# First attention of a two-layer kernel: the causal mask of the score tiles moves from TensorE matmuls into VectorE's row maximum of the diagonal tiles

## Chip, cores and metric

The kernel runs on one core of one Trainium2 chip, as one program. The metric is the device time of one execution in microseconds; the figure is the median of several runs. TensorE (PE in the profile) multiplies, VectorE (DVE) and ScalarE (ACT) work element by element, GpSimd (POOL) does element-wise work, masks and some transfers, SyncE (SP) issues most transfers.

## The reference, cut to what matters

Two layers stand in a row. Each computes `x + s * silu(g)`, with s an attention of the normalised x and g a feed-forward part. In the first layer s is a linear attention, and g holds a whole transformer block with a causal softmax attention of 16 heads of 16 dimensions, followed by a mixture of 8 experts. B is 2, T is 2048 and D is 256 there. That softmax attention is the "first attention" of the title:

```python
q, k = (rope(q), rope(k))
scores = jnp.einsum('bqhd,bkhd->bhqk', q, k) / math.sqrt(hd)
causal = jnp.tril(jnp.ones((Tt, Tt), dtype=bool))
scores = jnp.where(causal, scores, jnp.asarray(-1000000000.0, scores.dtype))
probs = jax.nn.softmax(scores, axis=-1)
attn = jnp.einsum('bhqk,bkhd->bqhd', probs, v).reshape(Bb, Tt, d) @ Wproj
```

The second layer has a causal attention too, of 16 heads of 32 dimensions.

## The kernel before, in words

The program's stages follow one another: projections for both attentions of layer one (`project_first`), the first attention (`narrow_attention`, L233), the expert layer, the projections of layer two, and the second attention (`wide_attention`, L763), which runs into the output.

**The work of the first attention.** The 2 x 16 heads are cut into 8 groups of 4 heads (HG). The 2048 queries are cut into 4 blocks of 512 (QB). A unit (g, u) is one group and one query block; its keys are blocks 0 to u. There are 32 units. For each unit two passes over the scores are made:

- *Score tiles* ("S", `score_tile`, L423): 128 queries on the partitions against up to 512 keys, written to one of three buffers `s_ps` (one bank each). VectorE takes the maximum over the keys (L393), which frees the buffer (`item_free`). Of a unit there are 4 x 4 x (u + 1) such tiles, 1280 in all. A tile with j == u is diagonal: it has only (qt + 1) x 128 columns, and its last 128 columns are cut by the causal mask. 512 tiles are diagonal, 128 of each width. The planner orders them by query tile, pair of heads, key block j and then head, so that the two diagonal tiles of a pair of heads follow one another. After a unit's tiles, "M" (L400 to L408) makes from the partial maxima a shift in two halves, and "T" transposes it into a strip which SyncE writes under the queries as two more rows.
- *Key tiles* ("ST", `key_tile`, L442): 128 keys on the partitions against the 512 queries, two heads per item, with the shift included. ScalarE takes the exponentials (L368), and "PV" (L510) multiplies them with the values: eight matmuls in single precision for four heads.

Two heads lie on partitions 0 to 49 and 64 to 113 (`heads_down` = 2), so matmuls of two heads use different rows of the array.

**The masks.** TensorE adds the causal mask itself. After the scores of a diagonal tile it multiplies an identity with a mask of -1e30 and adds into the last 128 columns, in two halves of 64 rows within the head's own half of the array:

```python
for half in range(2):
    wide = slice(64 * (1 - half), 64 * (1 - half) + P)
    mm = pe.matmul(place[:, width - P:width], ident_wide[rows, wide],
                   mask_wide[rows, wide], start=False, stop=half == 1)
```

Key tiles get theirs in the same way (L458) from `back_wide`. The wide masks are made by GpSimd in `NarrowMasks.make` (L218), long before the stage, and the constants in `make_constants` (L1138) at the start of the program.

The second attention treats its score tiles otherwise: there VectorE adds the mask `later` and takes the maximum in one instruction, `tensor_tensor_reduce` (L966), which appears in the trace as two records, an operation on the tile and a read of the accumulator.

**The order.** `narrow_schedule` (L62) writes out the order of all items ahead of time, and every engine follows it: TensorE issues S, ST and PV in the order of `body`, VectorE takes S, M and T in their order, and so on. It is made by a small model with costs per item: the start of each possible next item is computed, and the earliest goes next, an S item with a bonus of 100 ns. In this model a matmul costs 0.417 ns a column, a mask 110 ns, and a row maximum takes 1.04 ns a column plus 25 when VectorE is behind, or plus 125 after the tile's end plus 220 when it is idle (L160).

## Time and profile before

| | us |
|---|---|
| median of 3 runs (lowest, highest) | 3019.21 (3013.8, 3020.83) |
| span of the profiled execution, first to last instruction | 3006.4 |
| median of the runs above that span | 12.8 |
| the first attention, from its first row maximum to its last | 260 to 1041 |

The profiled execution has no time of its own beside its span; the 12.8 us lie before the first and after the last instruction of the program, or are the difference between executions. The profile lists busy time of each engine as the union of its records. A record runs from the start of an instruction to its modelled end, and records of successive instructions on one engine can overlap: the next may start before the record of the one before has ended. PEld are the weight loads of TensorE. PEclk is the share of TensorE's full clock that was granted.

### The profile page before, as it was taken

How to read it: one execution, taken by the hardware profiler on the slowest of the kernel's cores; microseconds unless marked ns; L12 is line 12 of the kernel's file. 1: busy time of each engine (PE TensorE's matmuls, PEld its weight loads, DVE VectorE, ACT ScalarE, POOL GpSimd, SP SyncE). 2: the span in 40 equal slices, each digit the busy share in tenths (PEclk: the TensorE clock that was granted, in tenths of full speed). 3: DMA queues.
4: the chain of work that ended last, by engine and by line, in shares of the span. 5: the costliest groups of instructions: out<-in, count | busy, mean ns of one | idle time of the engine just before them, and what ended most of it. 6: DMA issues, size and time to landing. Idle time of an engine off the chain costs nothing. (4 is left out here: it accounts for less than half of the span.)

```text
span 3006.4 us, 46248 instructions
## 1 busy us (share of the span) xinstructions
PE 2831.9 (94%) x18017; PEld 1317.3 (44%) x18017; DVE 2010.2 (67%) x4329; ACT 1545.3 (51%) x2581; POOL 990.0 (33%) x533
## 2 busy tenths in 40 slices
PE   7998999999999976999999899899999999999999
PEld 4664233333333344666676545323333333333327
DVE  7887899999999845000000565688787877878823
ACT  3452477676777755222222444345565665565571
POOL 1000000110101103111101330157777777777791
PEclk9997899999999987999999999889999999999999
DMA  4322122133202124232111466312020220202103
GB/s 130 97 77 76 37 51 39 43 62 66 50 24 62 24 68 130 63 86 75 63 48 34 148 193 185 79 32 61 8 64 12 68 64 8 64 12 68 67 12 119
DMA packets 141306, 200.77 MB, mean 67 GB/s; under 512 B 14320, under 2 KB 107904, under 8 KB 138000
## 3 DMA queue, kind: packets, MB, share of 16 engines
q1 hardware_dynamic: 130672, 173.21, 20.9%
q0 software_dynamic: 9056, 24.59, 3.9%
q8 instruction: 143, 2.34, 0.3%
q14 instruction: 75, 0.61, 0.1%
q10 hardware_dynamic: 1360, 0.01, 0.0%
HBM read 121.21 MB, written 76.02 MB: 66 GB/s over the span
## 5 line engine op out<-in xcount | busy, mean ns | idle before, releaser
L946 ACT ACTIVATE at_probs<-at_st 128x512 f32<-128x512 f32 (+3 forms) x1280 | 588.5, 542 | 442.1 <-PE at_st L1040 282.4
L909 POOL TENSOR_TENSOR at_probs<-at_probs 128x2048 f32<-128x2048 f32 (+3 forms) x205 | 725.9, 3546 | 214.7 <-ACT at_probs L946 135.4
L393 DVE TENSOR_REDUCE at_part<-at_s 128x1 f32<-128x512 f32 (+3 forms) x1280 | 690.0, 603 | 63.0 <-PE at_s L431 28.6
L368 ACT ACTIVATE at_probs<-at_st 128x1024 f32<-128x1024 f32 (+3 forms) x640 | 541.6, 895 | 275.4 <-PE at_st L450 141.0
L972 DVE TENSOR_REDUCE at_part<-at_s 128x1 f32<-128x512 f32 x768 | 498.5, 683 | 67.8 <-PE at_s L1032 63.9
L966 DVE CUSTOM_DVE_ANT_0 at_s<-at_s,at_later 128x384 f32<-128x384 f32 (+3 forms) x512 | 246.9, 498 | 103.8 <-PE at_s L1032 102.4
L510 PE MATMUL at_acc<-at_probs,at_v 128*32 128x512 f32 (+3 forms) x2560 | 305.5, 551 | 8.2 <-ACT at_otile L355 7.8
L2358 DVE TENSOR_TENSOR ex_ot<-ex_bank,lin_b 128x512 f32<-128x512 f32 x32 | 22.2, 692 | 426.3 <-PE ex_bank L2388 352.2
L2321 ACT ACTIVATE ex_hT<-ex_bank,ex_b 128x512 f32<-128x512 f32 x128 | 87.9, 687 | 334.7 <-PE ex_bank L2378 332.7
L2378 PE MATMUL ex_bank<-ex_xT,lin_w 128*128 128x512 f32 x512 | 225.5, 598 | 1.0 <-ACT ex_xT L2314 1.0
L2388 PE MATMUL ex_bank<-lin_w,ex_hT 128*128 128x256 f32 x1024 | 223.7, 379 | 0.8 <-ACT ex_hT L2321 0.8
L1032 PE MATMUL at_s<-all_k,all_q 96*128 96x512 f16 (+3 forms) x640 | 199.4, 366 | 15.1 <-DVE at_part L972 6.1
L2388 PEld LDWEIGHTS ex_bank<-lin_w,ex_hT 128*128 128x128 f32 x1024 | 193.9, 190 | 31.1 <-issue 3.8
L1040 PE MATMUL at_st<-all_q,all_k 98*128 98x512 f16 (+3 forms) x640 | 194.9, 362 | 6.6 <-ACT at_probs L946 3.8
L1032 PE MATMUL at_s<-at_kT,at_qT 96*128 96x512 f16 (+3 forms) x640 | 192.3, 356 | 8.3 <-DVE at_part L966 3.8
L431 PE MATMUL at_s<-lin_k_first,lin_q_first 48*128 48x512 f16 (+3 forms) x640 | 184.6, 374 | 14.9 <-DVE at_part L393 5.8
L1040 PE MATMUL at_st<-at_qT,at_kT 98*128 98x512 f16 (+3 forms) x640 | 185.1, 350 | 8.3 <-ACT at_probs L946 6.8
L431 PE MATMUL at_s<-at_kT,at_qT 48*128 48x512 f16 (+3 forms) x640 | 176.4, 361 | 6.9 <-DVE at_part L393 4.2
L1864 POOL DMA_DIRECT2D att_sums<-att x28 | 14.5, 523 | 487.7 <-DMA att<-at_otile 487.7
L2549 POOL DMA_INDIRECT p_rows<-exp_out,all_gather_at x64 | 62.1, 970 | 270.3 <-PE p_rot L2731 182.3
L2378 PEld LDWEIGHTS ex_bank<-ex_xT,lin_w 128*128 128x128 f32 x512 | 98.2, 192 | 118.2 <-issue 117.5
L1094 PE MATMUL at_acc<-at_probs,at_v 128*32 128x512 f32 (+3 forms) x1280 | 144.4, 536 | 4.0 <-ACT at_otile L928 3.8
(342 smaller groups left out, 3950.0 us busy)
## 6 DMA issues: line engine op xcount, KB each, us to landing
att<-at_otile SPq DMA_DIRECT2D x64, 256.0 KB, 2.1
lin_w<-in_W SPq DMA_DIRECT2D x16, 1024.0 KB, 7.5
at_v<-v SPq DMA_DIRECT2D x11, 1024.0 KB, 11.1
v<-pr_vt SPq DMA_DIRECT2D x32, 256.0 KB
exp_out<-ex_ot SPq DMA_DIRECT2D x32, 256.0 KB, 2.1
v<-p_vt SPq DMA_DIRECT2D x32, 256.0 KB, 3.7
p_xs<-in_x SPq DMA_DIRECT2D x8, 512.0 KB, 5.2
qhi<-p_parts SPq DMA_DIRECT2D x8, 512.0 KB
```

What stands on the lines that cost most here:

```text
L368: act.activation(probs[:, quad % RING, heads_down * p:heads_down * (p + 1), off:QB], st_ps[n % st_slots][:, :, off:QB], ACT.Exp, scale=EXP ...
L393: dve.tensor_reduce(part[:, w % 2, qt * HG + h, j:j + 1], s_ps[n % S_SLOTS][:, 0:width], AX.X, ALU.max).then_inc(item_free, 1)
L431: mm = pe.matmul(place[:, 0:width], QT[g % 2][rows, h // heads_down, q0:q0 + P], KT[g % 2][rows, h // heads_down, j * QB:j * QB + width], ...
L510: mm = pe.matmul(acc_ps[32 * h:32 * h + 32, off:QB], V[g % 2][:, kc, 32 * h:32 * h + 32], probs[:, quads % RING, h, off:QB], start=kc == 0 ...
L909: pool.tensor_tensor(total, total, probs[:, slots.slot[quad], :, off:QB], ALU.add).then_inc(add_done, 1)
L946: act.activation(probs[:, slots.slot[quad], h, off:QB], st_ps[n % ST_SLOTS][:, off:QB], ACT.Exp, scale=EXP_SCALE).then_inc(exp_done, 1)
L966: dve.tensor_tensor_reduce(out=s_ps[n % S_SLOTS][:, 0:width], in0=s_ps[n % S_SLOTS][:, 0:width], in1=later[:, QB - width:QB], scale=1.0, s ...
L972: dve.tensor_reduce(part[:, w % 2, qt * HG + h, j:j + 1], s_ps[n % S_SLOTS][:, 0:width], AX.X, ALU.max).then_inc(item_free, 1)
L1032: pe.matmul(place[:, 0:width], QT[g % 2][0:K, h, q0:q0 + P], KT[g % 2][0:K, h, j * QB:j * QB + width], start=True, stop=True).then_inc(ite ...
L1040: mm = pe.matmul(place[:, off:QB], KT[g % 2][0:K + 2, h, kc * P:(kc + 1) * P], QT[g % 2][0:K + 2, h, u * QB + off:(u + 1) * QB], start=Tru ...
L2378: mm = pe.matmul(d[:, :], w1[e % 2][:, n, f * P:(f + 1) * P], xT[:, n, cb * QB:(cb + 1) * QB], start=n == 0, stop=n == NF - 1)
L2388: mm = pe.matmul(d[:, t * D:(t + 1) * D], hT[cb][:, n, (2 * m + t) * P:(2 * m + t + 1) * P], w2[e % 2][:, n, :], start=n == 0, stop=n == N ...
```

## The change

The two mask matmuls of every diagonal score tile are left out. VectorE's row maximum of a diagonal tile becomes one `tensor_tensor_reduce`, which adds `later` (zeros, with -1e30 above the diagonal in its last 128 columns) to the tile in place and takes the maximum. Other tiles keep `tensor_reduce`. VectorE waits once, at the start of the stage, until the masks are made. The tile `mask_wide` and the constant `mask_qk` are not made any more (`mask_qk` was read by nothing), `later` is made in their place, and the counts of the semaphores follow. The key tiles' masks stay. In the planner, the 110 ns of a diagonal tile's mask go, and VectorE's cost, for plain and diagonal tiles alike, becomes 1.04 ns a column plus 125 after the later of the tile's end plus 220 and the end of VectorE's last item less 60: 1.04 ns a column plus 65 where VectorE is behind.

```diff
@@ -154,10 +154,10 @@
                 row_at[ev[1]] = dve + 2500
             else:
                 of_unit = of_unit + 1 if of_unit < count[ev[1]] else 1
-                end = start + ev[5] * COLUMN + (110 if ev[4] == ev[1][1] else 0)
+                end = start + ev[5] * COLUMN
                 issue, rows[ev[3] % heads_down] = start + 30, end
                 pe = max(pe, end)
-                dve = max(dve + ev[5] * 1.04 + 25, end + 220 + ev[5] * 1.04 + 125)
+                dve = max(dve - 60, end + 220) + ev[5] * 1.04 + 125
             slot_free[n_item % s_slots] = dve
             n_item += 1
             if at < len(ahead) and ahead[at][0] == "M":
@@ -212,16 +212,21 @@
 
 class NarrowMasks:
     def __init__(self, c):
-        self.tiles = [c.sb(n, [P, 3 * P // 2], BF16) for n in ("ident_wide", "mask_wide", "back_wide")]
+        self.tiles = [c.sb(n, [P, 3 * P // 2], BF16) for n in ("ident_wide", "back_wide")]
+        self.later = c.sb("later", [P, QB], BF16)
         self.cleared, self.ready = c.sem("masks_cleared"), c.sem("masks_ready")
 
     def make(self, pool):
-        for wide in self.tiles:
-            pool.memset(wide[:, :], 0.0).then_inc(self.cleared, 1)
+        for tile in (*self.tiles, self.later):
+            pool.memset(tile[:, :], 0.0).then_inc(self.cleared, 1)
         pool.wait_ge(self.cleared, 3)
+        last = self.later[:, QB - P:QB]
+        pool.affine_select(out=last, in_=last, compare_op=ALU.is_ge, fill=MASK, base=0, pattern=[[-1, P]],
+                           channel_multiplier=1).then_inc(self.ready, 1)
+        pool.wait_ge(self.ready, 1)
         for y in range(2):
-            for wide, compare, fill, base, step in zip(self.tiles, (ALU.not_equal, ALU.is_ge, ALU.is_ge),
-                                                       (1.0, MASK, MASK), (64, 64, -64), (-1, -1, 1)):
+            for wide, compare, fill, base, step in zip(self.tiles, (ALU.not_equal, ALU.is_ge),
+                                                       (1.0, MASK), (64, -64), (-1, 1)):
                 part = wide[64 * y:64 * y + 64, :]
                 pool.affine_select(out=part, in_=part, compare_op=compare, fill=fill, base=base,
                                    pattern=[[step, 3 * P // 2]], channel_multiplier=-step).then_inc(self.ready, 1)
@@ -380,6 +385,7 @@
         def _(dve):
             n, w = 0, 0
             due = []
+            dve.wait_ge(masks.ready, 5)
             for ev in body:
                 if ev[0] == "EV" and ev[1] == last_unit[ev[1][0]] and ev[1][0] + 1 < GROUPS:
                     due.append([ev[1][0], LATER])
@@ -389,9 +395,13 @@
                         A.invert(dve, due.pop(0)[0])
                 if ev[0] == "S":
                     _, (g, u), qt, h, j, width = ev
+                    place, to = s_ps[n % S_SLOTS][:, 0:width], part[:, w % 2, qt * HG + h, j:j + 1]
                     dve.wait_ge(item_ready, n + 1)
-                    dve.tensor_reduce(part[:, w % 2, qt * HG + h, j:j + 1],
-                                      s_ps[n % S_SLOTS][:, 0:width], AX.X, ALU.max).then_inc(item_free, 1)
+                    if j == u:
+                        dve.tensor_tensor_reduce(out=place, in0=place, in1=masks.later[:, QB - width:QB], scale=1.0,
+                                                 scalar=MASK, op0=ALU.add, op1=ALU.max, accum_out=to).then_inc(item_free, 1)
+                    else:
+                        dve.tensor_reduce(to, place, AX.X, ALU.max).then_inc(item_free, 1)
                     n += 1
                 elif ev[0] == "M":
                     g, u = ev[1]
@@ -423,20 +433,12 @@
             def score_tile(ev, n):
                 _, (g, u), qt, h, j, width = ev
                 q0 = u * QB + qt * P
-                diagonal = j == u
                 place = s_ps[n % S_SLOTS]
                 if n >= S_SLOTS:
                     pe.wait_ge(item_free, n - S_SLOTS + 1)
                 rows = slice(base(h), base(h) + K)
                 mm = pe.matmul(place[:, 0:width], QT[g % 2][rows, h // heads_down, q0:q0 + P],
-                               KT[g % 2][rows, h // heads_down, j * QB:j * QB + width],
-                               start=True, stop=not diagonal)
-                if diagonal:
-                    rows = slice(base(h), base(h) + 64)
-                    for half in range(2):
-                        wide = slice(64 * (1 - half), 64 * (1 - half) + P)
-                        mm = pe.matmul(place[:, width - P:width], ident_wide[rows, wide],
-                                       mask_wide[rows, wide], start=False, stop=half == 1)
+                               KT[g % 2][rows, h // heads_down, j * QB:j * QB + width], start=True, stop=True)
                 mm.then_inc(item_ready, 1)
 
             def key_tile(ev, n):
@@ -1127,20 +1129,20 @@
 def constants(nc, c, shift_rows):
 
     C = {"ident16": c.sb("ident16", [P, P], BF16), "ident_f16": c.sb("ident_f16", [P, P], F16),
-         "identf": c.sb("identf", [P, P], F32), "mask_qk": c.sb("mask_qk", [P, P], BF16),
+         "identf": c.sb("identf", [P, P], F32),
          "mask_kq": c.sb("mask_kq", [P, P], BF16), "ones32": c.sb("ones32", [P, 32], F32), "onesf": c.sb("onesf", [P, P], F32),
          "ones16": c.sb("ones16", [P, P], BF16), "tri16": c.sb("tri16", [P, P], BF16),
          "shift_rows": shift_rows, "const_ready": c.sem("const_ready")}
-    C["const_count"] = 15
+    C["const_count"] = 13
     return C
 
 
 def make_constants(pool, C):
-    for k in ("ident16", "ident_f16", "identf", "mask_qk", "mask_kq"):
+    for k in ("ident16", "ident_f16", "identf", "mask_kq"):
         pool.memset(C[k][:, :], 0.0).then_inc(C["const_ready"], 1)
     for k in ("ones32", "onesf", "ones16", "tri16"):
         pool.memset(C[k][:, :], 1.0).then_inc(C["const_ready"], 1)
-    pool.wait_ge(C["const_ready"], 9)
+    pool.wait_ge(C["const_ready"], 8)
 
     pool.affine_select(out=C["tri16"][:, :], in_=C["tri16"][:, :], compare_op=ALU.is_ge,
                        fill=0.0, base=0, pattern=[[1, P]],
...
@@ -1150,14 +1152,10 @@
                            fill=1.0, base=0, pattern=[[-1, P]],
                            channel_multiplier=1).then_inc(C["const_ready"], 1)
 
-    pool.affine_select(out=C["mask_qk"][:, :], in_=C["mask_qk"][:, :], compare_op=ALU.is_ge,
-                       fill=MASK, base=0, pattern=[[-1, P]],
-                       channel_multiplier=1).then_inc(C["const_ready"], 1)
-
     pool.affine_select(out=C["mask_kq"][:, :], in_=C["mask_kq"][:, :], compare_op=ALU.is_ge,
                        fill=MASK, base=0, pattern=[[1, P]],
                        channel_multiplier=-1).then_inc(C["const_ready"], 1)
-    pool.wait_ge(C["const_ready"], 15)
+    pool.wait_ge(C["const_ready"], 13)
 
 
 NT = B * T // P
```

The two hunks that are not shown drop `mask_wide` where `masks.tiles` is unpacked, and change the count that TensorE waits for from 6 to 5.

## Rows read from the trace of the kernel before

**Rows 1.** The page: busy time by engine, granted clock in 40 slices.

```profile
PE 2831.9 (94%) x18017; PEld 1317.3 (44%) x18017; DVE 2010.2 (67%) x4329; ACT 1545.3 (51%) x2581; POOL 990.0 (33%) x533
...
PEclk9997899999999987999999999889999999999999
```

**Rows 2.** Stretches: us, PE, PEld, DVE, ACT, POOL, PEclk, DMA share, GB/s.

```profile
400.00:500.00 100.00, 97.22 (x925) 35.74 (x924) 92.87 (x186) 69.50 (x85) 11.70 (x17) 1.00 0.25 50
500.00:600.00 100.00, 98.23 (x958) 37.50 (x960) 93.64 (x185) 71.17 (x87) 11.40 (x17) 1.00 0.25 50
...
700.00:800.00 100.00, 98.27 (x936) 36.83 (x936) 92.61 (x184) 70.88 (x86) 11.40 (x17) 0.98 0.25 50
...
260.00:1045.00 785.00, 758.55 (x6959) 281.53 (x6958) 721.44 (x1415) 522.34 (x630) 80.56 (x122) 0.96 0.23 46
```

**Rows 3.** Timeline of TensorE around 610 us: start, us, engine, line, what.

```profile
610.23 0.28 PE L431 MATMUL at_s<-at_kT,at_qT 48*128 48x256 f16 x1
610.35 0.27 PE L438 MATMUL at_s<-lin_mask_wide,lin_ident_wide 64*128 64x128 bf16 x2
```

**Rows 4.** Waits in 260 to 1045 us: who waited for whom, total, times, longest.

```profile
PEld at_s L431 <- DVE at_part L393: 328.2, 650, 1.7
...
DVE at_part L393 <- PE at_s L431: 28.6, 48, 2.0
DVE at_part L393 <- PE at_s L438: 23.2, 55, 4.9
```

**Rows 5.** By form, 255 to 1050 us: count, busy, mean ns, idle before.

```profile
L393 DVE TENSOR_REDUCE at_part<-at_s 128x1 f32<-128x512 f32 x896 | 562.7, 683 | 38.3 <-PE at_s L431 24.3 <-PE at_s L438 7.2
...
L438 PE MATMUL at_s<-lin_mask_wide,lin_ident_wide 64*128 64x128 bf16 x1024 | 133.2, 224 | 0.0
...
L438 PEld LDWEIGHTS at_s<-lin_mask_wide,lin_ident_wide 64*128 64x128 bf16 x1024 | 88.3, 99 | 25.3 <-issue 2.6
L393 DVE TENSOR_REDUCE at_part<-at_s 128x1 f32<-128x384 f32 x128 | 64.8, 548 | 4.3 <-PE at_s L438 4.1
...
L393 DVE TENSOR_REDUCE at_part<-at_s 128x1 f32<-128x256 f32 x128 | 48.6, 417 | 7.5 <-PE at_s L431 4.3 <-PE at_s L438 1.3
...
L393 DVE TENSOR_REDUCE at_part<-at_s 128x1 f32<-128x128 f32 x128 | 32.8, 284 | 13.0 <-PE at_s L438 10.6
```

**Rows 6.** Busy time by stretch, early in the stage, columns as in rows 2.

```profile
260.00:380.00 120.00, 109.21 (x781) 39.47 (x776) 104.24 (x204) 48.39 (x59) 1.77 (x4) 0.75 0.19 41
320.00:330.00 10.00, 8.34 (x35) 2.91 (x36) 8.89 (x19) 2.70 (x4) 0.00 (x0) 0.50 0.04 16
```

**Rows 7.** Timeline of VectorE, plain row maxima of the first attention.

```profile
312.42 7.27 DVE L393 TENSOR_REDUCE at_part<-at_s 128x1 f32<-128x512 f32 x12 [0.33 <-PE at_s L431]
...
876.93 0.68 DVE L393 TENSOR_REDUCE at_part<-at_s 128x1 f32<-128x128 f32 x3
```

**Rows 8.** Timeline of VectorE, masked row maxima of the second attention.

```profile
2234.08 0.69 DVE L966 CUSTOM_DVE_ANT_0 at_s<-at_s,at_later 128x512 f32<-128x512 f32 x1
2234.68 0.14 DVE L966 DVE_READ_ACCUMULATOR2_ANT at_part<- 128x1 f32 x1
2234.68 1.88 DVE L972 TENSOR_REDUCE at_part<-at_s 128x1 f32<-128x512 f32 x3
...
1908.67 0.73 DVE L966 CUSTOM_DVE_ANT_0 at_s<-at_s,at_later 128x512 f32<-128x512 f32 x1
1909.32 0.14 DVE L966 DVE_READ_ACCUMULATOR2_ANT at_part<- 128x1 f32 x1
1909.32 0.73 DVE L966 CUSTOM_DVE_ANT_0 at_s<-at_s,at_later 128x512 f32<-128x512 f32 x1
```

**Rows 9.** Timeline of GpSimd: a select of the constants, the last of the masks.

```profile
3.35 0.28 POOL L1153 TENSOR_SCALAR_AFFINE_SELECT all_mask_qk<-all_mask_qk 128x128 bf16<-128x128 bf16 x1
...
38.33 0.39 POOL L226 TENSOR_SCALAR_AFFINE_SELECT lin_back_wide<-lin_back_wide 64x192 bf16<-64x192 bf16 x1
```

**Rows 10.** One line's instructions: ns min/median/max, first and last start in us.

```profile
L393 DVE TENSOR_REDUCE at_part<-at_s x1280: 279/681/693, 260.2 to 1040.6; 128x1 f32<-128x512 f32 x127, 128x1 f32<-128x256 f32 x21, 128x1 f32<-128x128 f32 x19, 128x1 f32<-128x384 f32 x16
```

More of the change, by code:

```diff
@@ L260, in narrow_attention @@
         otile = c.sb("otile", [P, 2, QB], F32)
-        ident_wide, mask_wide, back_wide = masks.tiles
+        ident_wide, back_wide = masks.tiles
         st_ps = [c.ps(f"st{k}", [P, heads_down, QB]) for k in range(st_slots)]
@@ L462, in _ @@
             pe.wait_ge(C["const_ready"], C["const_count"])
-            pe.wait_ge(masks.ready, 6)
+            pe.wait_ge(masks.ready, 5)
             n = pairs = quads = 0
```

## Prediction, made before the changed kernel was run

> **What bounds the kernel now.** I read the page first: its slices and its busy shares say that TensorE is the fullest engine of the whole [rows 1]. Its chain of waits is of no use here: its lines are those of the second attention and of the end. So the first attention was cut out with the stretches. In 260 to 1045 us TensorE is busy 758.55 of 785 us and VectorE 721.44; ScalarE has 522.34 and GpSimd 80.56 [rows 2]. Two engines are nearly full, and the question is which one leads. TensorE's busy time overstates it, because a matmul's record outlasts its share of the array: in the example at 610 us the mask's record starts 0.12 us after a matmul whose own record is 0.28 us long [rows 3]. The waits settle it. The weight load of a score tile waits 650 times, 328.2 us together, for VectorE's row maximum to free one of the three score buffers, while VectorE waits for a score tile 48 + 55 times, 51.8 us in all [rows 4]. So VectorE leads: TensorE stands at the head of its queue until a buffer comes free, and VectorE stops only now and then, when the score tile was late. The planner's body alternates about four score tiles with two key tiles and one product with V, and eight matmuls of such a product cannot be interrupted. From the shapes, the stage gives VectorE 896 reductions of 512 columns and 128 of each narrower width [rows 5].
>
> **The change, part by part.**
>
> *TensorE's masks.* 1024 matmuls and 1024 weight loads leave, two for each of the 512 diagonal tiles [rows 5]. What counts is by how much a tile is ready earlier. In the example the tile's own matmul ends at 610.23 + 0.28 = 610.51 and its masks at 610.35 + 0.27 = 610.62 [rows 3]: 0.11 us. Since VectorE leads, this is worth something only where VectorE was waiting. Lower bound: the 55 waits that ended on a mask [rows 4], 55 x 0.11 = 6.1 us. Upper bound: diagonal tiles come in pairs (two heads), so in front of each of the 103 waits two of them may have pushed back what TensorE issued later: 103 x 2 x 0.11 = 22.7 us. I take the upper one, for two reasons. Where VectorE's records overlap by 0.085 us (below), waits shorter than that are not counted among the 103, and they shrink too. And at half clock (260 to 380 us has a granted clock of 0.75 on average [rows 6]) each mask costs double.
>
> *VectorE's plain reductions.* 12 of 512 columns in a row last 7.27 us, one 0.683: (7.27 - 0.68) / 11 = 0.60 us from start to start; three of 128 columns give (0.68 - 0.28) / 2 = 0.20 [rows 5, 7]. The next one starts 0.085 us before the end of the one before.
>
> *VectorE's diagonal tiles.* The new instruction is the one that the second attention already uses, on the same shapes, so its rows stand for it. It is two records, the operation and a read of the accumulator (0.14 us). Alone between reductions: started 2234.08, next reduction started 2234.68, 0.60, and the three reductions from there last 1.88 = 2 x 0.60 + 0.68: about 0.01 us more before and after at most [rows 8]. Behind another of its kind: 1908.67 to 1909.32, 0.65, so 0.05 more than 0.60 [rows 8]. For the 24 units with u > 0 that is 8 pairs each: 192 x (0.01 + 0.05 + 0.01) = 13.4 us. In the 8 units with u = 0 all 16 tiles are diagonal and follow one another: 8 x (0.01 + 15 x 0.05 + 0.01) = 6.2 us. The 32 row maxima (L400) also wait for the last accumulator read: between 0 and 32 x 0.14 = 4.5 us, taken at the middle, 2. Together **21.6 us** more work on the leading engine. From both sides: 13 (all singles and pairs at 0.04) to 24.
>
> What does a rule make of this? The row shows the accumulator read and the next operation starting at the same time, 1909.32 and 1909.32 [rows 8]. The Trainium skill (VectorE: DVE Perf Modes, "The DRAIN you can't avoid") says that the next operation does not start until the pipe of the one before is empty, and counsels few operations rather than fused ones. Read strictly it would make each diagonal tile cost the full 0.73 + 0.14 us instead of 0.65; the rows do not agree. The sum does not use it; it returns as a rival.
>
> *The buffer comes free later.* A reduction frees it after 0.68 us, the new pair of records after 0.60 + 0.14 = 0.74 (0.65 + 0.14 = 0.79 behind its like) [rows 8]. Waiting for that is TensorE's next score matmul but two, and behind it in the same queue the key tiles (so ScalarE's exponentials) and the products. As three buffers are in use, 0.06 to 0.11 us matter only where VectorE runs dry: at most 103 x 0.07 = 7.2 us. Against it, at the same waits, the tiles queued in front last 0.07 us longer on VectorE if a pair is among them, which hides as much: 103 x 0.07 = 7.2. I set the two off.
>
> *The order.* The planner's VectorE was 1.04 ns a column plus 25 when full, 0.557 us for 512 columns; the trace has 0.60. The changed formula gives 1.04 ns plus 65, 0.597. So the whole body is laid out anew with a truer VectorE for plain tiles (and 0.05 too fast for paired diagonal ones, and without their later release). No row shows what an order is worth. The nearest are the hundreds of the present one, each with other pieces of the pattern: VectorE is busy between 92.61 and 93.64 of 100 us [rows 2], 1.03 a hundred, or 8 us over 785. I take 0, from -8 to +8.
>
> *Preparation.* GpSimd loses one fill and one select of the constants (the select 0.28 us) and, in the masks, two selects for one (one of that kind takes 0.39), with a wider fill and one more wait; the last of them ends at 38.7 us [rows 9], and VectorE's new wait for `masks.ready` stands at 260 us. No DMA is added or moved, so no queue of SP or GpSimd is passed. Cost 0; were the cover gone, under 1 us.
>
> **Sum.** 21.6 - 22.7 = -1.1 us against the span of 3006.4 us. The median of the three runs is 3019.2, 12.8 more than the profiled span; that difference stays. So 3018 us. What a measurement of this kernel can tell from no change is about 0.2%, 6 us.
>
> **The rivals.**
>
> *Faster: the waits shrink more than that.* If the new cover hides (7.2) without the later release biting, and the truer order brings its 8: -1.1 - 7.2 - 8 = -16.3, **3003 us**. For it: VectorE's visible idle time is 785 - 721.44 = 63.6 us, and TensorE becomes looser by a good part of the masks' busy 133 us. Against: VectorE's own work is a floor that rises by 21.6.
>
> *Slower: VectorE leads and TensorE's relief is worth little.* Place: the row of diagonal tiles in each unit. If only the 55 mask-ended waits shrink, 21.6 - 6.1 = +15.5, **3035 us**. It decides from the point where less than 21.6 - 6 = 15.6 us of waiting disappears. For it: 650 waits of TensorE for VectorE against 103 the other way. Against: most waits of VectorE stand behind a product with V, with diagonal tiles just before, and these now take less of TensorE.
>
> *Slower: the clock.* In 320 to 330 us the granted clock is 0.50, the lower of the two levels (1.2 GHz), with TensorE busy 8.34 of 10; the hundreds with 97 to 98 have 0.98 to 1.00 [rows 2, 6]. With less to do TensorE could stay at the lower level longer. Price from either level: 204 VectorE operations in 120 us is 0.588 us each, and 186 in 100 us is 0.538, so 9%: one more such stretch of 120 us is worth 10 us, 3028. The Trainium skill (TensorE: Matmul & The Clock Gate, "What's actually happening") has activity release the throttle; the trace agrees that the fuller stretches have the full clock.
>
> *The strict rule on emptying.* Each diagonal tile would take its whole record and the read after it: at 512 columns 0.69 to 0.73, say 0.70, and 0.14 [rows 8], so 0.24 us over a reduction's 0.60, and as much at the other widths, x 512 = 123 us, 3141. The rows speak against it.
>
> *The change does not do what it says:* masks that ran wholly beside other matmuls free nothing. That is the slower rival with 21.6 instead of 15.5, 3041, and is counted there.
>
> **How the numbers follow.** Cancelling, as forecast: 0.42 (of it 0.02 beyond the bound on either side). Faster: 0.36. VectorE's bound: 0.17. Clock: 0.04. Strict rule: 0.01. So faster by over 0.2%: 0.36 + 0.02 = 0.38; within: 0.38; slower: 0.17 + 0.04 + 0.01 + 0.02 = 0.24. Both signs hold much, so the forecast's own range is given too: 3018 - 8 to 3018 + 8 for the order, 3010 to 3026. The range for 8 in 10 reaches to the faster rival, 3003, and most of the way to the slower one, 3033.
>
> **What would show each step.** Gone: all 1024 mask matmuls. VectorE: 512 pairs of records in place of as many reductions, 0.60 us apart at 512 columns alone and 0.65 behind one another; if the second is 0.60, 10 us of the cost were not real. Waits of VectorE for a score tile in the stage: from 51.8 us to about 30 as forecast; below 20 the faster rival, above 40 the slower one. Waits of TensorE's weight load for VectorE should grow from 328 us, since TensorE gets looser. The stage's start, 260 us, stays; its last row maximum over a score tile, now at 1040.6 [rows 10], tells the change by itself. The rest of the kernel should move as a block: any difference there is not of this change. The forecast is wrong if the stage moves by more than 8 us either way.

## The result, and the profile after

The changed kernel takes 3035.4 us (median of four runs, 3035.3 to 3041.1), the one before 3017.0 us in its four: the ratio is 1.0071, 95% interval 1.0056 to 1.0086. It is 18 us slower, 2 us above the range that was given. It fell where the slower rival had been put (3035). That the number agrees is luck: VectorE got less added work than that rival has (16.9 us and not 21.6), its waits grew where the rival lets them shrink, and some 8 us came back at the stage's end. Two executions in the batch of a5 and a6, one of a5 at 5298.8 us and one of the kernel before at 10281.7 us, lie far outside the others and are in no ratio below.

One correction to the frame comes first. The profiled execution of the changed kernel took 3035.48 us for a span of 3033.7, so only 1.8 us lie around a span; in the kernel before it is 2.1 (one of its executions has 3008.55 us for a span of 3006.4). By that, the execution of the kernel before that was profiled (span 3006.4) took some 3008.5 us, and was one of its fastest: its runs beside the later experiments lie between 3008.6 and 3022.7. The 12.8 us that the prediction took to be around the span were mostly difference between executions. So the traces, 27.3 us apart, show 9 us more than the medians do.

The page of the changed kernel, busy shares and granted clock in 40 slices:

```profile
PE 2830.3 (93%) x16993; PEld 1268.7 (42%) x16993; DVE 2032.9 (67%) x4841; ACT 1544.8 (51%) x2581; POOL 989.7 (33%) x530
...
PEclk9997799999999897999999899899999999999999
```

The 1024 matmuls are gone, and VectorE has 512 records more (the accumulator reads). The span grew in the first attention: its last row maximum ends at 1073.7 us instead of 1041.3, its last eviction at 1107.5 instead of 1083.5, and the second attention starts 27.0 us later and takes 1102.7 instead of 1102.4 us. The 8 us between the first two differences come back at the stage's end: from the last row maximum to the last eviction it takes 33.9 us instead of 42.2. That belongs to the order: the kernels below in the changed order have 33 to 35 us there, those in the former order 41 to 43, as the changed order leaves less key work behind the last score tile.

Stretches of the changed kernel (us, PE, PEld, DVE, ACT, POOL, PEclk, DMA share, GB/s), to be laid beside [rows 2]:

```profile
260.00:1078.00 818.00, 762.84 (x5998) 233.55 (x5997) 743.84 (x1927) 530.62 (x639) 81.86 (x123) 0.90 0.22 44
400.00:500.00 100.00, 92.89 (x750) 28.80 (x748) 89.15 (x222) 67.47 (x82) 11.68 (x17) 0.90 0.25 48
500.00:600.00 100.00, 94.36 (x795) 29.94 (x792) 93.33 (x244) 69.45 (x85) 11.42 (x17) 0.95 0.25 51
700.00:800.00 100.00, 94.40 (x788) 29.86 (x788) 92.97 (x243) 69.32 (x84) 11.40 (x17) 0.93 0.26 50
```

The granted clock in the stage is 0.90 where it was 0.96, and it is 0.90 to 0.95 in hundreds that had 0.98 to 1.00 [rows 2]. Summed over the trace's records of the clock, the stage has 169 us at the lower level instead of 74.

The waits of the changed kernel in 260 to 1078 us:

```profile
PEld at_s L440 <- DVE at_part L404: 248.8, 435, 1.7
PEld at_s L440 <- DVE at_part L401: 141.8, 306, 1.7
DVE at_part L404 <- PE at_s L440: 36.9, 61, 2.2
...
DVE at_s L401 <- PE at_s L440: 25.3, 48, 4.8
```

VectorE's visible waits are 62.2 us in 109 times, against 51.8 in 103 [rows 4]. They were to fall to 30. TensorE's weight load waits 390.6 us for VectorE instead of 328.2, as expected from a looser TensorE.

VectorE's records at the end of the stage, start and duration in us:

```profile
1058.21 0.69 DVE L401 CUSTOM_DVE_ANT_0 at_s<-at_s,lin_later 128x512 f32<-128x512 f32 x1
1058.81 0.14 DVE L401 DVE_READ_ACCUMULATOR2_ANT at_part<- 128x1 f32 x1
1058.81 0.73 DVE L401 CUSTOM_DVE_ANT_0 at_s<-at_s,lin_later 128x512 f32<-128x512 f32 x1
1059.46 0.14 DVE L401 DVE_READ_ACCUMULATOR2_ANT at_part<- 128x1 f32 x1
1059.46 1.28 DVE L404 TENSOR_REDUCE at_part<-at_s 128x1 f32<-128x512 f32 x2
```

From one start to the next it is 0.60 for the first of a pair, 0.65 for the second, and 0.60 for the plain ones after it (1.28 less 0.68): the distances of [rows 8], to the hundredth.

**Work and waits of VectorE.** For all that follows the stage was split by VectorE's records. The least distance from one start to the next is 598, 465, 332 and 198 ns for plain tiles of the four widths, 8 more for a masked one, 51 more for a masked one behind another, 7 more for a plain one behind it, and fixed values for the small operations. What a start comes later than that is a wait; the rest is work. The order of VectorE's own items is the same in every kernel here (but for the seven divisions by the sums), so any two can be compared item by item. What the two "orders" differ in is where TensorE puts the score tiles between its key tiles and products.

| kernel | masks on TensorE | row maximum | order | median us | ratio to before, 95% | work | waits | low clock |
|---|---|---|---|---|---|---|---|---|
| before | yes | plain | former | 3017.0 | 1 | 705.2 | 79.5 | 74 |
| changed | no | masked | changed | 3035.4 | 1.0071 (1.0056 to 1.0086) | 722.1 | 93.0 | 169 |
| a4_fill_old | load only | masked | former | 3036.1 | 1.0063 (1.0039 to 1.0088) | 723.1 | 84.2 | 99 |
| a1_ttr_old | no | masked | former | 3041.8 | 1.0099 (1.0081 to 1.0118) | 724.7 | 87.1 | 150 |
| a5_none_old | no | plain | former | 3013.2 | 0.9993 (0.9982 to 1.0004) | 706.6 | 77.0 | 116 |
| a6_none_new | no | plain | changed | 3030.5 | 1.0046 (1.0030 to 1.0062) | 707.0 | 99.8 | 173 |
| a2_red_new | yes | plain | changed | 3054.1 | 1.0140 (1.0122 to 1.0158) | 705.2 | 126.0 | 154 |
| a3_fill_new | load only | masked | changed | 3059.2 | 1.0156 (1.0139 to 1.0173) | 722.1 | 116.2 | 150 |

Work and waits in us from the first row maximum over a score tile to the end of VectorE's last copy of the stage (1.6 to 4.6 us after the last such maximum); low clock in us at 1.2 GHz up to the last eviction. "Load only" means that TensorE does the mask matmuls but the scores overwrite them. The ratios are each to the kernel before in the same batch. Every kernel has one profile here, and a profile differs from the next by up to 10 us, as the repeats below show.

### The profile page after: what moved, and what is told of

It is laid out like the page before. It is cut to its first block and busy times, and to the rows that moved or that the text cites. A ratio compares the mean times of both kernels' runs of the same rounds, so it can differ in the third digit from the quotient of the medians.

```text
span 3033.7 us, 44708 instructions
## 1 busy us (share of the span) xinstructions
PE 2830.3 (93%) x16993; PEld 1268.7 (42%) x16993; DVE 2032.9 (67%) x4841; ACT 1544.8 (51%) x2581; POOL 989.7 (33%) x530
## 5 line engine op out<-in xcount | busy, mean ns | idle before, releaser
L974 DVE TENSOR_REDUCE at_part<-at_s 128x1 f32<-128x512 f32 x768 | 498.4, 683 | 68.2 <-PE at_s L1034 64.3
L404 DVE TENSOR_REDUCE at_part<-at_s 128x1 f32<-128x512 f32 x768 | 484.4, 684 | 42.1 <-PE at_s L440 36.9
L512 PE MATMUL at_acc<-at_probs,at_v 128*32 128x512 f32 (+3 forms) x2560 | 315.6, 565 | 7.4 <-ACT at_otile L360 7.4
L401 DVE CUSTOM_DVE_ANT_0 at_s<-at_s,lin_later 128x384 f32<-128x384 f32 (+3 forms) x512 | 242.5, 510 | 29.6 <-PE at_s L440 25.3
L440 PE MATMUL at_s<-lin_k_first,lin_q_first 48*128 48x512 f16 (+3 forms) x640 | 192.5, 389 | 27.6 <-DVE at_part L404 16.9
L440 PE MATMUL at_s<-at_kT,at_qT 48*128 48x512 f16 (+3 forms) x640 | 186.0, 381 | 16.6 <-DVE at_part L404 12.1
L1096 PE MATMUL at_acc<-at_probs,at_v 128*32 128x512 f32 (+3 forms) x1280 | 144.4, 536 | 4.0 <-ACT at_otile L930 3.8
```

The lines of the kernel that those rows point to most:

```text
L404: dve.tensor_reduce(to, place, AX.X, ALU.max).then_inc(item_free, 1)
L440: mm = pe.matmul(place[:, 0:width], QT[g % 2][rows, h // heads_down, q0:q0 + P], KT[g % 2][rows, h // heads_down, j * QB:j * QB + width], ...
L512: mm = pe.matmul(acc_ps[32 * h:32 * h + 32, off:QB], V[g % 2][:, kc, 32 * h:32 * h + 32], probs[:, quads % RING, h, off:QB], start=kc == 0 ...
L974: dve.tensor_reduce(part[:, w % 2, qt * HG + h, j:j + 1], s_ps[n % S_SLOTS][:, 0:width], AX.X, ALU.max).then_inc(item_free, 1)
L1096: mm = pe.matmul(acc_ps[32 * h:32 * h + 32, off:QB], V[g % 2][:, kc, 32 * h:32 * h + 32], probs[:, slots.slot[quads], h, off:QB], start=kc ...
```

## The experiments

Three theories were set against one another. W: VectorE's added work sets the time. O: the order that the changed planner writes costs it. C: TensorE, relieved of the masks, gets the lower clock for longer. The change has three parts (masks off TensorE, masked row maximum, order), and the first six experiments make the other six combinations of them.

**a1_ttr_old**: the changed kernel with the former planner.

```diff
-                dve = max(dve - 60, end + 220) + ev[5] * 1.04 + 125
+                dve = max(dve + ev[5] * 1.04 + 25, end + 220 + ev[5] * 1.04 + 125)
```

(and the 110 ns of a mask back in `end`.)

> The changed kernel, but with the order of the kernel before (its planner put back). Theory W (VectorE's 20 us of added work set the time): 3035, as the changed kernel. Theory O (the new order costs it): back to 3017, within 5. Theory C (without the masks TensorE's granted clock falls in a stretch of every group): it depends on whether this order also leaves TensorE a thin stretch; if it does, some stretches of 10 us at 0.5 and about 3030; if not, the clock is 0.99 to 1.00 in 400 to 1000 us and the time is 3017 to 3022.

3041.8 us. O falls as it stood: giving the changed kernel its former order back does not return its loss. By the medians that order is even 6 us worse for it (ratios 1.0099 and 1.0071, whose intervals just overlap).

**a2_red_new**: the kernel before with the changed planner; the diff above the other way round.

> The kernel before (masks on TensorE, plain row maxima), but in the order of the changed planner. Theory W: 3017, since VectorE's work is the old one. Theory O: 3030 or more, most of the loss is there. Theory C: the masks keep TensorE occupied, so the clock stays near 1.00 in 400 to 1000 us and the time is within 5 of 3017.

3054.1 us, 42 above its batch's kernel before. W and C, which gave 3017 within 5, fall here. So for the kernel before, the changed order is far worse: 46.5 us more waits for the same work. Its waits of VectorE for score tiles:

```profile
DVE at_part L393 <- PE at_s L438: 50.9, 77, 4.9
DVE at_part L393 <- PE at_s L431: 47.0, 77, 2.2
```

97.9 us against 51.8 [rows 4]. What an order is worth is not a matter of 8 us. The lower clock comes with the order too: 154 us instead of 74, although TensorE has all its masks.

**a3_fill_new** and **a4_fill_old**: the changed kernel and a1, in which TensorE does the two mask matmuls of each diagonal tile ahead of the scores, which overwrite them.

```diff
+                if j == u:
+                    rows = slice(base(h), base(h) + 64)
+                    for half in range(2):
+                        wide = slice(64 * (1 - half), 64 * (1 - half) + P)
+                        pe.matmul(place[:, width - P:width], ident_wide[rows, wide],
+                                  back_wide[rows, wide], start=half == 0, stop=half == 1)
```

> The changed kernel with two mask matmuls ahead of each diagonal score tile, whose result the scores overwrite: TensorE has its old load again, VectorE keeps the new one. Theory C: the clock returns to 0.98 to 1.00 in 400 to 1000 us and the time falls below the changed kernel's 3035, to about 3022. Theory W: 3035 plus up to 22 for the later tiles, 3035 to 3057. Theory O: 3035 or more.

> The same two overwritten mask matmuls, changed VectorE work, and the order of the kernel before: only VectorE's instruction on diagonal tiles differs from the kernel before. Theory W: 3017 + 20 = 3037. Theory O: 3017. Theory C: clock near 1.00, 3017 plus what VectorE's added work costs by itself, between 5 and 20.

a3 takes 3059.2 us, 24 more than the changed kernel, and its low stretches stay (150 us): in the changed order they do not come from the missing masks. a4 differs from the kernel before in VectorE's instruction and in that the mask matmuls stand ahead of the scores instead of behind them: 17.9 us more work, 4.7 more waits, and 3036.1 us against 3012.2 in its batch. That is W's term in the former order, and it is as large as the loss of the whole change (1.0039 to 1.0088 against 1.0056 to 1.0086). In the changed order the same term is much smaller, as a6 shows.

**a5_none_old** and **a6_none_new**: neither mask (plain row maxima over unmasked diagonal tiles, with sums floored so that the output stays finite), in both orders.

```diff
+        dve.tensor_scalar(self.sums[:, :], self.sums[:, :], 1.0e-30, None, ALU.max).then_inc(self.floored, 1)
+        dve.wait_ge(self.floored, g + 1)
         dve.reciprocal(self.sums[:, :], self.sums[:, :]).then_inc(self.inverted, 1)
```

> Neither the two mask matmuls nor the masked row maximum: plain row maxima over unmasked diagonal tiles (so the shift may come from a later key, and the sums are floored at 1e-30), order of the kernel before. It shows what taking the masks off TensorE does alone. Theory C (less load on TensorE brings the lower clock): low stretches spread over the stage as in the run with the old order and the masked maximum, no gain, 3012 to 3022. Theory G (the relief is worth its 22 us and VectorE's work ate it): 2990 to 2998.

> The same without both masks, in the changed planner's order, which has in each group one run of 11 score tiles with no key tile and no product between. Against the changed kernel it leaves out VectorE's added work alone. Theory W: 20 us below the changed kernel, 3015. Theory C: also about 3015, but with one low stretch of 10 to 14 us in each group at the same places.

a5: 3013.2 us, ratio 0.9993 with an interval that holds 1 (0.9982 to 1.0004, so at most 5 us gained). In the former order, taking all masks off TensorE's score tiles gains nothing that can be told; VectorE pays only 1.4 us for it, the seven floors of the sums. The 22 us that its expectation calls theory G are not there. VectorE's one kind of wait there:

```profile
DVE at_part L393 <- PE at_s L431: 51.5, 78, 4.7
```

51.5 us against 51.8 before [rows 4]: fewer, and longer. Item by item against the kernel before, 104 of the items at full clock in both wait 17.5 us less (the relief is real), 50 wait 13.8 us more, and the items that fell into a low stretch wait 8.2 instead of 2.1, while those that came out of one wait 4.0 less. It is more than chance: between the first profile of the kernel before and its repeats, 4 or 5 items at full clock wait 1 to 2 us less and 8 to 10 wait 3 to 5 more.

a6 takes 3030.5 us with 173 us at low clock, where both W and C had 3015. In it VectorE waits 72.9 us:

```profile
DVE at_part L393 <- PE at_s L431: 72.9, 125, 4.7
```

So the changed order costs 17 us over a5 (ratios 0.9993 and 1.0046) with no mask anywhere, and the masked row maxima, 15.1 us more work on top of it, only 5 us more by the medians and 8 by the ratios (1.0046 and 1.0071), as waits fall from 99.8 to 93.0.

The eight kernels together say that the three parts do not add. What each part adds to the time, in per cent, from the ratios (each has an interval of 0.1 to 0.25 to either side):

| part | in which kernels | former order | changed order |
|---|---|---|---|
| masked row maximum | masks still on TensorE | +0.63 | +0.16 |
| masked row maximum | masks off TensorE | +1.06 | +0.25 |
| masks off TensorE | plain row maximum | -0.07 | -0.94 |
| masks off TensorE | masked row maximum | +0.36 | -0.85 |

The changed order adds 1.40 (masks on, plain), 0.93 (load only, masked) and 0.53 (no mask), and takes 0.28 off in the whole change. So the loss of 0.71% has no single owner: which part seems to bring it depends on the part that one starts with.

**b1_runfill_after**, **b2_runfill_red_new**, **b3_prefill_after** try to hold the clock by filling TensorE. Reading the two orders as written showed what stands where the changed one has a low stretch in each group: it has, in groups 1 to 7, a run of 9 to 11 score tiles with no key tile and no product with V between, while the former order has none past group 0 or 1. Key tiles of a unit need its row maxima turned and stored; in the changed order the key tiles have caught up (lead 1.67 units on average against 1.88), and nothing else is left to do. In the changed kernel's timeline the run looks so (chosen records):

```profile
648.57 0.23 PE L440 MATMUL at_s<-at_kT,at_qT 48*128 48x128 f16 x1 [0.25 <-DVE at_part L401]
...
649.84 0.23 PE L440 MATMUL at_s<-at_kT,at_qT 48*128 48x128 f16 x1 [1.05 <-DVE at_part L404]
...
652.17 0.28 PE L440 MATMUL at_s<-at_kT,at_qT 48*128 48x128 f16 x1 [0.49 <-DVE at_part L404]
...
654.80 1.03 PE L452 MATMUL at_st<-at_qT,at_kT 50*128 50x512 f16 x4 [0.24 <-DMA at_qT<-at_strip]
...
655.51 1.02 ACT L373 ACTIVATE at_probs<-at_st 128x1024 f32<-128x1024 f32 x1 [10.24 <-PE at_st L452]
```

ScalarE had nothing for 10.24 us. The stretches around it:

```profile
640.00:650.00 10.00, 8.38 (x86) 3.26 (x86) 9.60 (x23) 3.29 (x7) 0.00 (x0) 1.00 0.01 2
650.00:660.00 10.00, 7.77 (x36) 2.19 (x35) 9.17 (x28) 4.26 (x5) 2.36 (x5) 0.53 0.23 76
660.00:670.00 10.00, 9.88 (x62) 2.15 (x54) 7.69 (x21) 5.88 (x7) 5.08 (x5) 0.78 0.25 33
```

By the trace's records of the clock it falls to 1.2 GHz at 650.7 us, within the run, and is back at 664.4. In the run itself VectorE is busy 9.17 to 9.60 of 10: it loses little there. The key tiles come at 654.8, still at the lower clock. In 660 to 670 us, of which 4.4 are at the lower clock (0.78 on average), TensorE is busy 9.88 and VectorE only 7.69.

```diff
+                if n in filled:
+                    for x in range(4):
+                        pe.matmul(place[:, x * P:(x + 1) * P], C["ident16"][:, :], C["mask_kq"][:, :],
+                                  start=True, stop=True)
```

`filled` holds the tiles of the runs in b1 and b2, and in b3 the 512-column plain ones among the 12 items before a run.

> The changed kernel with four idle matmuls of 128 columns, overwritten by the scores, ahead of each score tile of the runs of 11 in groups 1 to 7, where TensorE only waits for VectorE. Theory C: the low stretch of each group after that run (7 of 10 to 14 us) goes, the clock in 400 to 1000 us is 0.98 or more, and the time falls by 8 to 20 us, to 3015 to 3027. If the clock is not what costs, the time stays at 3035 or rises by up to 5 while the clock recovers.

> The same filling in the kernel before with the changed order (3054 without it). Theory C: clock 0.98 or more in 400 to 1000 us and 3025 to 3040. If the order costs by its interleaving and not by the clock, it stays at 3050 or more.

> The changed kernel with four idle matmuls of 128 columns, overwritten by the scores, ahead of the plain 512-column score tiles among the 12 items before each run of score tiles without key tiles. There VectorE has two wide tiles queued, so the 0.21 us each should hide, unlike in the run itself, where it showed in full. Theory C: the low stretches near 450, 550, 650 us and so on (10 to 14 us each, 7 of them) vanish or shorten, VectorE's waits at low clock fall from 38 us by 10 to 17, and the time from 3035 to 3018 to 3026. Theory O alone: the clock recovers and the time stays at 3033 to 3038.

3051.7, 3059.4 and 3062.7 us: all worse, and none does what it was for. In b1 the low stretches stay (169 us), and the filling runs at the lower level:

```profile
658.39 0.61 PE L452 MATMUL at_s<-all_mask_kq,all_ident 128*128 128x128 bf16 x4
658.93 0.10 PEld L455 LDWEIGHTS at_s<-at_kT,at_qT 48*128 48x128 f16 x1 [0.20 <-issue]
658.93 0.28 PE L455 MATMUL at_s<-at_kT,at_qT 48*128 48x128 f16 x1
659.14 0.35 PEld L452 LDWEIGHTS at_s<-all_mask_kq,all_ident 128*128 128x128 bf16 x4
...
660.01 0.30 DVE L401 CUSTOM_DVE_ANT_0 at_s<-at_s,lin_later 128x128 f32<-128x128 f32 x1 [0.40 <-PE at_s L455]
```

Four idle matmuls take 0.54 us before each score matmul (658.39 to 658.93), more than VectorE spends on a narrow tile, so it waits. b3 adds 26 us of waits at full clock. b2 does lift the clock (101 us low instead of 154) but pays for it with the filling. By b2's expectation a time over 3050 would speak for the interleaving and against the clock. But as tests of the clock all three failed: filling a tile's own path is not free, and what it costs cannot be told from what the clock gives back. So no experiment here separates the price of the long runs from that of the lower clock behind them.

**c1_ttr_own40**, **c2_red_dve60**, **c3_ttr_no110** are other orders: c1 and c3 for the changed work, c2 for the kernel before. c1 adds 40 ns for a diagonal tile to the former formula, c3 only drops the 110 ns of the masks, c2 takes the changed VectorE formula and keeps them.

> The changed kernel's work in an order from the former planner with 40 ns added for each diagonal tile and the 110 ns of the mask kept, as if TensorE still had it. This order keeps the lead of the score tiles at 1.87 units (former order 1.88, changed one 1.67) and has no run of over 5 score tiles. Theory C: as the changed work in the former order, thin load spread over the stage, 120 to 150 us at low clock, 3035 to 3042. If the order's fit to VectorE's added work matters more than the clock: 3025 to 3032.

> The kernel before, whose planner gets the changed formula for VectorE but keeps the 110 ns of the masks. With both changed it took 3054. If the loss there came from planning without masks that TensorE still had to do, 3015 to 3025 here; if it came from the VectorE formula (lead 1.72, runs of 9 score tiles), 3040 to 3055.

> The changed kernel's work in an order from the former VectorE formula without the 110 ns of the masks: the planner knows TensorE's lighter load and believes VectorE 7% faster than it is. Lead 1.77, one run of 9 at the end. Theory C: fewer and shorter low stretches than the changed kernel's 169 us, 100 to 140, and 3022 to 3032. Theory W alone: 3035.

3049.5, 3046.1 and 3038.4 us. c2 says that most of a2's loss (waits 116.2 us where a2 has 126.0 and the kernel before 79.5) comes with the VectorE formula, though this formula is the truer one by [rows 7]. c1 kept the lead at 1.87 and had no long run, and still had 186 us at low clock, spread in 3 to 17 us pieces: the run is one way to the lower clock, not the only one. c1 came out 7 us above what its expectation allowed, and c3 (159 us at low clock) missed the 3022 to 3032 of C. Four orders were tried on the masked row maximum with TensorE relieved: the changed kernel's (1.0071), c3's (1.0074), the former one (1.0099) and c1's (1.0106). The first two cannot be told apart, and none comes within 0.5% of the kernel before.

**The repeats.** d1 and d2 are the kernel before, d3 is a5, d4 the changed kernel, each profiled again without an edit. They bear on the clock's price, as nothing was edited between them.

> The kernel before, profiled once more. If the lower clock costs time, an execution whose stage has more than 74 us at low clock is longer, by about 0.15 us for each us, with the extra waits of VectorE at the items that fell into the low stretches. If the clock costs nothing, the stage stays at 781 us whatever the low stretches do.

> The kernel before, profiled a third time, for a second pair of executions that differ in the clock alone. If the lower clock costs time, the stage grows by about 0.15 us for each us at low clock; otherwise it stays at 781 us.

> The run without either mask in the former order, profiled once more (116 us at low clock, 780 us the first time). By the clock's price of 0.15 us for each us the two profiles differ by their difference in low clock.

> The changed kernel, profiled once more. Its run of 11 score tiles in each group should again be followed by a low stretch of 10 to 14 us at the same items, since the cause lies in the order and not in chance; stage 813 us within 5.

| profile | low clock | work | waits | last row maximum ends after |
|---|---|---|---|---|
| before | 73.6 | 705.2 | 79.5 | 781.1 |
| d1 | 88.7 | 705.1 | 84.3 | 785.9 |
| d2 | 70.6 | 706.1 | 79.2 | 781.6 |
| a5 | 116.1 | 706.6 | 77.0 | 779.9 |
| d3 | 132.6 | 706.1 | 86.9 | 789.4 |
| changed | 168.8 | 722.1 | 93.0 | 813.4 |
| d4 | 174.1 | 723.0 | 95.4 | 816.7 |

Low clock, work, waits and the last column are in us, the last counted from the first row maximum. 15.1 us more at low clock went with 4.8 us more of stage (0.32 each), 16.5 with 9.5 (0.58), 5.3 with 3.3 (0.62). From d2 to d1 it is 18.1 with 4.3 (0.24), and d2, with 3.0 us less than the first profile, took 0.5 us longer. The record has more: over the 88 executions of all kernels with a span and a mean clock on record, those of one kernel compared with one another, each further us at the lower level goes with 0.30 us of span, give or take 0.03. The expected 0.15 was probably too low. These are executions that differ by themselves, so the figure says what goes together and not what the clock alone does. It can be seen in one stretch, first the kernel before, then d1:

```profile
810.00:820.00 10.00, 9.99 (x90) 3.20 (x91) 9.40 (x17) 7.85 (x9) 0.00 (x0) 1.00 1.01 209
```

```profile
800.00:900.00 100.00, 97.97 (x906) 35.82 (x902) 88.72 (x176) 69.60 (x85) 11.41 (x17) 0.95 0.22 50
...
810.00:820.00 10.00, 10.00 (x53) 2.01 (x53) 6.81 (x13) 4.97 (x7) 0.00 (x0) 0.67 0.94 164
```

VectorE does 176 operations in d1's hundred, and the kernel before does 184 in the same hundred at full clock (93.35 us busy): 8 operations, 4.3 us, with 10.2 us of the hundred at the lower clock. In d4 the low stretches stand at the same places as in the first profile of the changed kernel (451.5, 553.9, 652.9 against 449.3, 551.7, 650.7 us, and so on), so there they belong to the order.

## Why the prediction was wrong

**VectorE's added work: right, a little large.** The term was 21.6 us; the changed kernel has 16.9 us more work, a4 17.9 and a1 18.1 over a5. The distances read from the second attention held. Three small things made the rest: hundredths rounded up (8, 51 and 7 ns for 10, 50 and 10), the row maxima's wait for the last accumulator read, taken at 2 us where it came to about 1, and pairs that a wait breaks up, whose second tile then costs 8 ns and not 51. The prediction counts 312 tiles directly behind their like; the changed kernel has 224 of them, a1 271.

**TensorE's relief, with the order at nothing: the step that failed.** The relief was put at 22.7 us, the upper bound, and the order at 0, within 8. Together they were to take 22.7 us of waiting away. a6 has these two parts and no other, and its waits are 20.3 us longer than before (99.8 against 79.5); with the masked row maxima they are 13.5 us longer (93.0). The 0.11 us for one tile's masks was not the mistake: where both mask matmuls follow their score matmul directly in the trace of the kernel before, they end a median 0.11 us after it at full clock and 0.21 at the lower one. Taken apart, the relief depends on the order. With former order and plain maxima it came to 2.5 us of waits (a5), and with masked ones to -2.9 (a4 to a1): nothing. In the changed order it is indeed 26.2 and 23.2 us (a2 to a6, a3 to the changed kernel). The bound counted masks ahead of waits; it did not ask whether the order had been fitted around them. The former planner did count 110 ns for each mask; that it had thereby put them where VectorE was not short is the likely reason and is not shown. What is shown is that the relief is paid back item by item in a5: 17.5 us of waits less at some items, 13.8 more at others, and 6.1 more at those that fell into the 42 us more of lower clock.

**The clock: foreseen, but mostly from another cause, with too small a size and a chance of 0.04.** Waits at low clock rose from 17.3 to 38.3 us, and at full clock fell from 62.1 to 54.7. That is where the 13.5 us of added waits are. The rival has TensorE at the lower level for longer because it has less to do. In the former order that adds 42 us (a5). Of the changed kernel's 95 us, though, the order alone brings 80 (a2, with all masks in place), and taking the masks off adds 19 to it (a2 to a6, a3 to the changed kernel). The prediction took the price from 260 to 380 us against a later hundred, 10 us for 120 at an average clock of 0.75 [rows 6], so 60 us low: 0.17 for each, where the repeats show 0.24 to 0.62 and all executions together 0.30. And it feared one more such stretch, 60 us, where 95 came. What the 95 us cost stays open. By 0.30 they are worth 28 us, and the relief and the order would have given back some 15. But VectorE waits 0.25 us in each us at the lower level and 0.09 in each at full clock in the kernel before, and 0.24 and 0.08 in the changed one. By that difference of 0.16, 95 us more at the lower level are worth 15 us, the whole rise of the waits, and nothing was given back. Both are worked out and not measured.

The Trainium skill (TensorE: Matmul & The Clock Gate, "What's actually happening") has activity release the throttle. The trace agrees for the runs of score tiles: 8.38 of 10 us busy, then a clock of 0.53. It does not explain d1's stretch at 810, ahead of which TensorE was busy 9.80 of 10; the cause of that one stays open.

**The order: the bound of 8 us was not one.** Hundreds of one order say nothing of another order. Between the two, waits differ by 46.5 us (masks on, plain), 32.0 (load only, masked), 22.8 (none, plain) and 5.9 (none, masked). The nearer the work is to what the changed planner assumes, the less its order costs. In waits it is not ahead even at the best; in time it is then, by 6 us of the medians (the changed kernel against a1), with the 8 us less at the stage's end on its side.

**The rivals.** The slower one gave 3035 by 21.6 - 6.1. Its size is right by luck, but the decision point holds: less than 15.6 us of waits disappeared, namely none. The reason it gave, that the relief is worth little, holds in the former order; in the changed one the relief is worth 23 us of waits, and the order takes more than that. The strict rule on emptying the pipe needs 0.84 us where 0.65 is seen above, and is ruled out. What would have been seen was listed rightly: waits above 40 for the slower rival; they are 62.

**The frame.** With 2.1 us around the span instead of 12.8, and the profiled execution known to be a fast one, the forecast would have been made against medians between 3012 and 3017.

## What to carry to other kernels

Where two engines are nearly full and an order is written out by a planner, taking work off the one that does not lead is worth what an experiment with that work simply left out shows, and here, in the order that was in place, that was nothing. Work moved onto the leading engine cost at least itself in the order that was in place: 18 us of it cost 19 and 32 us of time, by the ratios. In the changed order, which had already lost 20 to 46 us to waits, 15 to 17 us of it cost 5 and 8. An order fits the durations that it was planned with: edit the kernel and the planner in separate runs, and look for stretches in which the planner gives TensorE only one kind of work, as in this kernel the lower clock came with each of these and stayed on when the load returned.

## What the runs showed of the hardware

- Executions of one unchanged program differ in where the clock falls: 70.6, 73.6 and 88.7 us at the lower level in the same stage, and 781 to 786 us for it. Repeated profiles of one kernel give an estimate of the clock's price without an experiment: 0.24 to 0.62 us of stage for each us between pairs of profiles, and 0.30 of span over 88 executions.
- In the changed order the lower clock is felt late: VectorE is busy 9.17 of 10 us in the stretch where the clock falls, and 7.69 in the next, in which the key tiles' load is back.
- An accumulator read of 0.14 us costs the next plain operation under 0.01 us and the next masked one 0.05, in both attentions alike.
